# Two cross attentions: a copy moved ahead of an exponential, a split alignment, a third score bank in one, and band masks by matrix products in the other

## The reference

```python
def _L0_xattn_ref(mask, encodings, w_in, b_in, w_out, b_out, w_ct, b_ct, local_size):
    x = jnp.transpose(mask, (0, 2, 1))
    q, k, v = jnp.split(x @ w_in.T + b_in, 3, axis=-1)
    ...
    scores = jnp.einsum('bqhd,bkhd->bhqk', q, k) / jnp.sqrt(jnp.asarray(d, q.dtype))
    band = jnp.abs(idx[:, None] - idx[None, :]) <= local_size
    scores = jnp.where(band[None, None], scores, neg)
    attn = jax.nn.softmax(scores, axis=-1)
    o = jnp.einsum('bhqk,bkhd->bqhd', attn, v).reshape(n, t, e)
    o = jnp.transpose(o @ w_out.T + b_out, (0, 2, 1))
    y = jax.nn.relu(o) * encodings
    return jnp.einsum('nit,io->not', y, w_ct) + b_ct[None, :, None]

def _L1_xattn_ref(q, k, v):
    ...
    qk = jnp.einsum('bdm,bdn->bmn', qh, kh) * scale
    sm = jax.nn.softmax(qk, axis=-1)
    ret = jnp.einsum('bmn,bcn->bcm', sm, vh)
    return ret.reshape(b, c, m)
x = x + _L0_xattn_ref(_layernorm(x), ctx_2048, ..., 64)
...
x = x + _L1_xattn_ref(_layernorm(x), ctx_2048, ctx_2048)
```

## Time and profile before

| what | value |
|---|---|
| runs | 2758.41 us median of 3 (2756.8 to 2758.96) |
| profiled execution | 2778.94 us, span 2776.9 us |
| PE busy in the span | 2217.8 us (80%) |
| DVE busy | 1868.5 us (67%) |
| ACT busy | 1154.9 us (42%) |
| banded stage | some 393 to 1030 us, a pair every 19.62 us |
| full stage | some 1790 to 2360 us, a pair every 17.22 us |

### The profile page before, as it was taken

How to read it: one execution, slowest core, us unless ns; L and a number is a source line. 1 busy time by engine, 2 the same in 40 slices (tenths; PEclk the granted TensorE clock), 3 DMA queues, 4 the chain that set the end, 5 groups by cost and what they waited for, 6 DMA issues and landing times. The chain is left out here.

```text
span 2776.9 us, 55137 instructions
## 1 busy us (share of the span) xinstructions
PE 2217.8 (80%) x19084; PEld 1573.4 (57%) x19084; DVE 1868.5 (67%) x5654; ACT 1154.9 (42%) x2616; POOL 892.0 (32%) x1488
## 2 busy tenths in 40 slices
PE   4787739999989982999959999388888888378796
PEld 3676626666666652999947777144444444245453
DVE  4999967787878767555526666478788786334245
ACT  1222215555555542222216666066666665132232
POOL 3565532222222214666630000232222221324422
PEclk9888859999999995999979999599999999589898
DMA  3000033333333310000030000533333331123434
GB/s 110 1 0 1 1 98 90 95 87 94 86 94 84 94 37 0 2 2 2 2 149 1 2 2 2 142 101 102 101 101 101 101 102 49 44 65 94 135 107 157
DMA packets 252306, 183.16 MB, mean 66 GB/s; under 512 B 29056, under 2 KB 246304, under 8 KB 251264
## 3 DMA queue, kind: packets, MB, share of 16 engines
q1 hardware_dynamic: 240416, 156.52, 20.4%
q0 software_dynamic: 7456, 18.92, 1.9%
q10 hardware_dynamic: 4160, 4.19, 0.5%
HBM read 94.47 MB, written 83.51 MB: 64 GB/s over the span
## 5 line engine op out<-in xcount | busy, mean ns | idle before, releaser
L764 ACT ACTIVATE xattn_pr<-ps 128x384 f32<-128x384 f32 (+1 forms) x1024 | 544.3, 542 | 459.6 <-PE ps L499 260.0
L483 PE MATMUL ps<-xattn_kp,xattn_qp 96*128 96x192 bf16 (+1 forms) x2048 | 375.0, 265 | 99.1 <-DVE xattn_mx L634 38.3
L496 PE MATMUL ps<-xattn_qp,xattn_kp 128*128 128x192 bf16 (+1 forms) x2048 | 412.0, 263 | 3.3 <-ACT xattn_pr L764 2.7
L634 DVE TENSOR_REDUCE xattn_mx<-ps 128x2 f32<-128x512 f32 x512 | 333.5, 678 | 119.7 <-PE ps L483 117.7
L514 PE MATMUL ps<-xattn_pr,xattn_vs 128*32 128x256 f32 (+1 forms) x4096 | 307.2, 372 | 35.1 <-ACT xattn_o L769 34.9
L630 DVE CUSTOM_DVE_ANT_0 xattn_masked<-ps,xattn_band 128x192 bf16<-128x192 f32 x1024 | 324.2, 354 | 13.2 <-issue 5.7
L496 PEld LDWEIGHTS ps<-xattn_qp,xattn_kp 128*128 128x128 bf16 x2048 | 178.7, 97 | 171.7 <-issue 91.1
L483 PEld LDWEIGHTS ps<-xattn_kp,xattn_qp 96*128 96x128 bf16 x2048 | 175.5, 99 | 176.7 <-DVE xattn_mx L630 60.6
L499 PE MATMUL ps<-xattn_band,xattn_ident 128*128 128x192 bf16 x1024 | 211.2, 247 | 0.0
L1002 PE MATMUL ps<-ffn_parts,gate_up_t 128*128 128x128 bf16 x3072 | 194.7, 220 | 2.1 <-DVE ffn_parts L1120 2.1
L1002 PEld LDWEIGHTS ps<-ffn_parts,gate_up_t 128*128 128x128 bf16 x3072 | 184.5, 99 | 16.4 <-DVE ffn_parts L1120 2.5
(11 more groups left out here) (304 smaller groups left out, 4548.6 us busy)
## 6 DMA issues: line engine op xcount, KB each, us to landing
xattn_rows<-xattn_parts SPq DMA_DIRECT2D x128, 192.0 KB, 2.1
xattn_qp<-xattn_rows SPq DMA_DIRECT2D x256, 96.0 KB, 2.8
xattn_kp<-xattn_rows SPq DMA_DIRECT2D x256, 96.0 KB, 3.1
xattn_rows<-xattn_parts SPq DMA_DIRECT2D x128, 128.0 KB, 2.1
moe_rows_in<-region_zero SPq DMA_DIRECT2D x6, 1677.0 KB, 7.4
moe_xb<-moe_rows_in SPq DMA_DIRECT2D x78, 129.0 KB
xattn_rows<-xattn_parts SPq DMA_DIRECT2D x128, 64.0 KB, 1.8
moe_row<-moe_rows_out SPq DMA_DIRECT2D x16, 512.0 KB, 8.4
```

What stands on the lines that cost most here:

```text
L483: mm = nc.tensor.matmul(ps[:, BANK_S + j % RING, mt * D:mt * D + width], qp[u][s][0:R_MAX, h, mt * P:(mt + 1) * P], kp[u][s][0:R_MAX, h, l ...
L496: mm = nc.tensor.matmul(out, kp[u][s][:, h, nt * P:(nt + 1) * P], qp[u][s][:, h, lo:lo + width], start=True, stop=not banded)
L634: ins = nc.vector.tensor_reduce(mx[s][:, h * NT:(h + 1) * NT], ps[:, BANK_S + j % RING, :].rearrange("p (m n) -> p m n", m=NT), AX.X, ALU.max)
L764: nc.scalar.activation(out, src, ACT.Exp, scale=HD ** -0.5).then_inc(exped, 1)
```

## The change

In both stages: `keep_o` goes ahead of the exponential of the same step on ACT; `align` becomes four quarters, two at j = 4 and two at j = 5, with the denominators made first; the reciprocals move to j = 7 and 8, `normal_o` to 9. In the full stage scores have three banks in turn (0, 1 and 7), and `new_x` moves from j = 10 to 11. In the banded stage heads with odd h are masked on PE, by the product that `make_scores_t` uses already, and DVE takes their maxima with one plain reduction over 384 columns, without the small memset and without the wait for the head before; `gate_product` moves from j = 10 to 11.

```diff
-    BANK_S, BANK_T, BANK_O, BANK_N, BANK_PREP, BANK_END = 0, 2, 4, 5, 6, 7
+    BANK_T, BANK_O, BANK_N, BANK_PREP, BANK_END = 2, 4, 5, 6, 7
     TURNS = 2 * QUADS
+    ALIGNED = 4, 5
+
+    SCORES = (0, 1) if banded else (0, 1, BANK_END)
...
+        def masked_by_product(h):
+
+            return h % 2 == 1
...
-                    wait(pe, maxed, idx(p, j) - RING + 1)
+                    wait(pe, maxed, idx(p, j) - len(SCORES) + 1)
                     for mt in range(NT):
                         lo = mt * BAND if banded else 0
-                        mm = nc.tensor.matmul(ps[:, BANK_S + j % RING, mt * D:mt * D + width], qp[u][s][0:R_MAX, h, mt * P:(mt + 1) * P],
-                                              kp[u][s][0:R_MAX, h, lo:lo + width], start=True, stop=True)
+                        out = ps[:, SCORES[idx(p, j) % len(SCORES)], mt * D:mt * D + width]
+                        by_product = banded and masked_by_product(h)
+                        mm = nc.tensor.matmul(out, qp[u][s][0:R_MAX, h, mt * P:(mt + 1) * P],
+                                              kp[u][s][0:R_MAX, h, lo:lo + width], start=True, stop=not by_product)
+                        if by_product:
+                            mm = nc.tensor.matmul(out, ident16[:], band16[:, mt, :], start=False, stop=True)
...
-                def align(p):
-                    pe.wait_ge(o_kept, p + 1)
-                    wait(pe, normal, nth(p - 1, 3, 3))
-                    for sums in range(2):
-                        for half in range(2):
-                            at = C_SELECT + (2 * sums + half) * P
-                            mm = nc.tensor.matmul(ps[:, BANK_N, sums * D:(sums + 1) * D], c[:, at:at + P], o_sb[:, half, :],
-                                                  start=(half == 0), stop=(half == 1))
-                    mm.then_inc(aligned, 1)
+                def align(p, quarter):
+
+                    sums, half = 1 - quarter // 2, quarter % 2
+                    if quarter == 0:
+                        pe.wait_ge(o_kept, p + 1)
+                        wait(pe, normal, nth(p - 1, 3, 3))
+                    at = C_SELECT + (2 * sums + half) * P
+                    mm = nc.tensor.matmul(ps[:, BANK_N, sums * D:(sums + 1) * D], c[:, at:at + P], o_sb[:, half, :],
+                                          start=(half == 0), stop=(half == 1))
+                    if half == 1:
+                        mm.then_inc(aligned, 1)
...
-                        if j == 4 and not first:
-                            align(p - 1)
+                        if j in ALIGNED and not first:
+                            for half in range(2):
+                                align(p - 1, 2 * ALIGNED.index(j) + half)
...
-                        if banded and not first and j == 10:
+                        if banded and not first and j == 11:
                             gate_product(p - 1)
...
-                    if banded:
+                    if banded and not masked_by_product(h):
                         wait(v, maxed, idx(p, j))
                     v.wait_ge(scores, idx(p, j) + 1)
...
                     else:
-                        ins = nc.vector.tensor_reduce(mx[s][:, h * NT:(h + 1) * NT], ps[:, BANK_S + j % RING, :].rearrange("p (m n) -> p m n", m=NT),
-                                                      AX.X, ALU.max)
+                        of = ps[:, bank, :].rearrange("p (m n) -> p m n", m=NT)[:, :, 0:width]
+                        ins = nc.vector.tensor_reduce(mx[s][:, h * NT:(h + 1) * NT], of, AX.X, ALU.max)
...
-                    v.wait_ge(aligned, p + 1)
+                    v.wait_ge(aligned, nth(p, 2, 2))
...
-                        if j in (6, 7) and not first:
-                            reciprocal_sums(p - 1, j - 6)
-                        if j == 8 and not first:
+                        if j in (7, 8) and not first:
+                            reciprocal_sums(p - 1, j - 7)
+                        if j == 9 and not first:
                             normal_o(p - 1)
-                        if j == 10 and not first and not banded:
+                        if j == 11 and not first and not banded:
                             new_x(p - 1, 1 - u)
...
                     for j in range(NHS):
+                        if j == 2 and not first:
+                            keep_o(p - 1)
                         ahead = next_head(p, u, j + RING)
                         if there(ahead[0]):
                             exponentials(ahead[0], ahead[2])
                         if j == 0:
                             keep_maxima(p, u, 1)
-                        if j == 2 and not first:
-                            keep_o(p - 1)
```

More of the change, by code:

```diff
@@ L610, in _ @@
                 multiply(PAIRS - 1, 1, TURNS - 1)
-                align(PAIRS - 1)
+                for quarter in range(4):
+                    align(PAIRS - 1, quarter)
                 if banded:
@@ L622, in maxima @@
                         wait(v, max_parts, nth(run(p - 1, s), 4, 4))
-                    if banded:
+                    if banded and not masked_by_product(h):
                         wait(v, maxed, idx(p, j))
                     v.wait_ge(scores, idx(p, j) + 1)
-                    if banded:
+                    bank = SCORES[idx(p, j) % len(SCORES)]
+                    if banded and not masked_by_product(h):
                         nc.vector.memset(tick[:], 0.0)
@@ L630, in maxima @@
                             ins = nc.vector.tensor_tensor_reduce(
-                                out=masked[:, mt, :], in0=ps[:, BANK_S + j % RING, mt * D:mt * D + WIN], in1=band16[:, mt, :],
+                                out=masked[:, mt, :], in0=ps[:, bank, mt * D:mt * D + WIN], in1=band16[:, mt, :],
                                 scale=1.0, scalar=-BIG, op0=ALU.add, op1=ALU.max, accum_out=mx[s][:, h * NT + mt:h * NT + mt + 1])
                     else:
-                        ins = nc.vector.tensor_reduce(mx[s][:, h * NT:(h + 1) * NT], ps[:, BANK_S + j % RING, :].rearrange("p (m n) -> p m n", m=NT),
-                                                      AX.X, ALU.max)
+                        of = ps[:, bank, :].rearrange("p (m n) -> p m n", m=NT)[:, :, 0:width]
+                        ins = nc.vector.tensor_reduce(mx[s][:, h * NT:(h + 1) * NT], of, AX.X, ALU.max)
                     ins.then_inc(maxed, 1)
@@ L767, in keep_o @@
                     a.wait_ge(multiplied, TURNS * (p + 1))
-                    wait(a, aligned, p)
+                    wait(a, aligned, nth(p, 2, 0))
                     nc.scalar.activation(o_sb[:].rearrange("p a b -> p (a b)"), ps[:, BANK_O, :], ACT.Copy).then_inc(o_kept, 1)
```

## The result

The changed kernel takes 2692.8 us (median of 4 runs, 2689.5 to 2693.3), against 2758.05 of the kernel before in the same comparison: ratio 0.9761, 95% interval 0.9744 to 0.9778. The profiled execution took 2692.82 us, span 2690.8.

What follows compares the result with a forecast made beforehand. PE sets the pace, held up by partners' waits; banded -15 us (-0.47 a pair) and full -49 (-1.52 a pair), each times 32, make -64 from 2758.4: 2694 us, own range 2675 to 2714, with the next two rivals 2670 to 2738.

Steps and rivals of the forecast that it cites:

- five waits: Banded pair of the kernel before: three for maxima, one for ACT's copy, one for gated values, 2.5 us of 19.62.
- The split: Alignment in two halves of 0.87 us: both banded waits behind the reciprocals, 0.9 us with tails, taken as gone.
- behind the addition: Banded wait for a maximum behind the addition to x and its statistics: about 0.5 us stays of 0.7.
- for the gated values: Banded wait of PE between gate product and output product, through DVE's multiplication: 0.32 us becomes 0.2 to 0.3.
- the weights' load: Rival: weight loads beside the banded mask products not hidden, 0.08 us more each, +42 us, total 2736; chance 0.02.
- The rival that the products eat the banded gain: Removed waits return for gate and addition: banded pair 20.0 us, +13 us, total 2722; chance 0.17.
- PE's busy time: Sign of the forecast: PE's busy time up by about 42 us by 512 products.
- the tails: A matmul's modelled end hangs over into the wait, so each wait costs 0.12 to 0.16 us more than its bracket.
- Behind the reciprocals: Two banded PE waits, 0.36 and 0.20 us, for maxima after DVE's two reciprocals: both taken as gone.
- steps 13 and 15: Full stage, three banks played forward: PE waits for maxima only there, 0.3 and 0.6 us.
- SP's chain: Full stage, turning product to last row load landing, 11.75 us; rival if 1 us longer: pair 16.7, total 2726; chance 0.07.
- The slower rival: PE's added 1.33 us a banded pair comes whole and maxima waits stay: banded +42, full -22, 2778 us; chance 0.08.

Runs made afterwards that it cites:

- products alone: Kernel before with only the mask products and plain reductions for odd heads in the banded stage (denominators first in the alignment): 2759.6 us, ratio 1.0005.

## Why the prediction was right

The forecast was 2694 us and the time is 2692.8. The terms behind it held too, stage by stage, but the closeness of the total is partly luck: one cost was put at nothing, and errors of both signs cancelled.

*PE's pace.* PE's own work plus five waits was the right account: banded 18.43 + waits forecast 0.75, 19.15 to 19.2; measured 19.01. Full 14.5 + 0.9, taken as 15.7; measured 15.61. Stages: -15 forecast, -17.7 measured; -49 forecast, -47.1 measured. The factor 32 was too large: in the full stage 29 intervals between alignments shrank from 17.22 to 15.61, and the last two, 24.9 us together before, took 25.5. That took back 4.4 of the 51.5 us that 32 pairs would have given, while the pair was 0.09 us shorter than forecast, worth 2.9.

*The split.* The prediction gave each half of the alignment 0.87 us on PE, so nothing for splitting it. It costs 0.11 a pair in both stages, some 7 us in all. With it the banded pair adds up: 18.43 + 0.11 + 0.39 behind the addition + 0.09 for the gated values = 19.02, 19.01 measured.

*Products.* The trace shows them 0.08 us apart, 512 more in the whole kernel (19596 instructions on PE in place of 19084); the weights' load stayed hidden, so that rival falls. That they are not worth it in this company was not said: the prediction counted them at +1.33 and credited waits to the split and the products together. The experiments part them: 0.7 of waits saved for 1.33 beside the split, 1.26 for 1.33 without. The rival that the products eat the banded gain put the pair at 20.0 and falls by its number, but its thought was half right: the pair would have gained 1.24 without them and gained 0.61 with them.

*PE's busy time.* It was to rise by about 42 us, a sign that did not come: it rose by 18.5 (2217.8 to 2236.3), +1.06 a banded pair and -0.31 a full one, while the products alone raised it by 38 (to 2255.9). The likely reason is the one told of the tails: the part of a modelled end that reaches into a wait counts as busy, and goes with the wait. No run isolates it.

*The reduction.* 550 ns between the rows of 312 and 512 values, 547 measured; 0.47 to the next, 0.48 measured. DVE was to go from 15.5 to about 14 us a pair; its busy time went to 14.53, 0.9 less and not 1.6.

*Waits.* Behind the reciprocals: gone, as said. For the copy: gone in both; with the copy put back the full stage's loss was the 0.7 of the prediction. For the gated values: 0.25 forecast; the output product starts 0.56 us after a multiplication that takes 0.47, about 0.1. Behind the addition: 0.5 forecast, 0.22 and its tail 0.17, 0.39 measured. Both errors together are some 0.26; the split's 0.11, not forecast, leaves the 0.14 by which the banded pair was over-estimated.

*The full stage.* The waits stand at steps 13 and 15 with 0.27 and 0.38, 0.43 and 0.54 with tails, against 0.3 and 0.6 worked out. Beside the third bank the split saved none of it: the waits sum to the same without it. The prediction let the bank and the split work together and did not ask what each gave.

*SP's chain.* It was put at 11.75 us and came to 10.2; why it is shorter was not looked into. PE waited for a load once in 400 us, 0.2 us, so that rival falls. The allowance of some 0.2 us a pair for it and for the turned maxima looks nearly right only by luck: the 0.11 of the split stands in its place.

*The slower rival.* It needed the maxima waits to stay whatever the products do. Products alone show the opposite: the waits fell by 1.26 us, nearly PE's load of 1.33.

## What to carry to other kernels

Before an edit buys time for a partner engine with work of the engine that sets the pace, reorder the partner's queue: moving the addition and statistics behind the maxima that PE asks for first was worth 24 us, while the mask products cost 17 beside the split alignment. Cutting a run of products in two is not free either: it cost PE 0.11 us a pair, in the full stage for nothing. Two edits that remove the same wait must be tested apart, since each looks worth its price alone. And count the pace engine from start to start: with the later addition five waits in a banded pair showed no idle bracket at all.

## What was not expected of the hardware

- The product of gated values and the context took 1073 ns on average before (27 in the stretch from 414 to 966 us) and 954 now (28), with the same shapes and operands.

```profile
L667 DVE TENSOR_TENSOR xattn_y<-xattn_gate,xattn_ctx 128x256 f32<-128x256 f32 x27 | 29.0, 1073 | 2.8
```

```profile
L683 DVE TENSOR_TENSOR xattn_y<-xattn_gate,xattn_ctx 128x256 f32<-128x256 f32 x28 | 26.7, 954 | 3.3 <-DVE xattn_gate L680 0.5
```

GpSimd's timeline tells what goes with it. Each of the long ones begins while GpSimd works on `xattn_rest`, and ends 0.27 to 0.29 us after it (GpSimd's spans are rough); before:

```profile
700.35 1.07 DVE L667 TENSOR_TENSOR xattn_y<-xattn_gate,xattn_ctx 128x256 f32<-128x256 f32 x1
```

```profile
699.98 1.16 POOL L839 TENSOR_TENSOR xattn_rest<-xattn_qk,xattn_parts 128x512 f32<-128x512 f32 x1 [8.11 <-ACT xattn_parts L787]
```

The overlap is 0.79 us of 1.07 there, 0.69 of 0.97 in the changed kernel (GpSimd from 692.07, DVE from 692.54) and 0.65 of 0.92 without products. In the last four pairs of the banded stage, where no instruction of GpSimd runs beside it, the same product takes 0.42 to 0.43. So it hardly advances while GpSimd's instruction runs, and loses 0.5 to 0.65 us a pair; it stands between the gate product and the output product, for which PE waited 0.39 us before. No kernel with GpSimd's instruction elsewhere was run, so what that would be worth stays open.

- The 18 us by which the untouched mixture of experts differed between two profiled executions; its cause stays open.
